# A transformer block on one core: batches in loop passes, and the same work as sixteen slots of head groups

## The chip, the core and the metric

The kernel runs on one core of one Trainium2 chip. The metric is the device time of one execution in microseconds. TensorE does matmuls, VectorE and ScalarE elementwise work and the evacuation of PSUM banks, GpSimd elementwise work in SBUF alone, and SyncE issues all DMAs. In the profile they are PE (PEld for its weight loads), DVE, ACT, POOL and SP.

## What is computed

Four batches of 512 tokens of width 512, all in float32, one pre-norm transformer block with a ternary feed-forward part:

```python
x = x + attn(layernorm(x), Wqkv, Wo)      # 16 heads of 32, causal, softmax
x = x + ffn(layernorm(x), w1, w3, w2)
# attn: scores = q @ k^T * 32**-0.5; where(causal, scores, -1e9); softmax; @ v; @ Wo
# ffn:  s = mean(|w|); wq = clip(round(w / s), -1, 1) * s   for w1, w3 (1365x512), w2 (512x1365)
#       (silu(x @ w1q^T) * (x @ w3q^T)) @ w2q^T
```

## The kernel before

**Numbers in two halves.** Each float32 operand of a large product is kept as two 16-bit floats, high and low. ScalarE writes the high half out of the bank, VectorE subtracts it from the bank and writes the low half (`turned_high` and `turned_low`, `place`, L607, L800, L808). A product of q, k, v or project then has 4 blocks x 3 terms = 12 matmuls of 512 columns (L999, L1030). The ternary weights need one half only: gate and lin have 8 matmuls, down 22 for each tile of 128 tokens (L1139).

**Attention, by groups of four heads.** A batch has four groups. For each, q and k are computed as 128 x 512 tiles (four heads of 32 rows). Their halves are stacked along the partitions, three times 32 rows for each head, so that one matmul computes all three terms: `q_stack` and `k_stack`. ScalarE copies the high half of each head into the first rows (L625), VectorE the low half (L817), and SyncE copies the first rows to a second place within SBUF (`stack`, L456, L457). Work on scores goes in ten *units* of 512 columns a group, which hold the sixteen (head, tile of 128 rows) pairs of causal widths 512, 384, 256 and 128; two units are a *piece*. There are two passes over the scores:

- `scores`: queries on partitions, two banks in turn. A matmul for each pair (L1056) and a second one that adds a large negative triangle to its last 128 columns (L1058, `mask_rows` and `mask_cols`). VectorE reduces each unit to block maxima (L829), and four small operations make the row maxima of them (L836 to L840). These are transposed (`max_row`, L1066), split, and sent by two small DMAs into two more rows of the q stack, against rows of ones (times 32768) in the k stack.
- `probs`: keys on partitions, the same products with the maximum subtracted by the extra rows (L1083), exponentials on ScalarE (L642), and GpSimd sets what is above the diagonal to zero (`select`, L558, three operations for each half of the heads).

`values` then multiplies the probabilities with v and, again, with ones for the sums (L1102, sixteen float32 products each), into `o_bank` and `sum_bank`. VectorE takes the reciprocal (L844) and the product (L850), ScalarE and GpSimd split the result (L647, L563). `project` multiplies with Wo and VectorE adds to the residual `x_res` (L856).

**The feed-forward part.** `gate` and `lin` alternate over eleven chunks of 128 hidden rows: tanh on ScalarE (L657), two scalar_tensor_tensor on VectorE (L864, L875), the halves on ScalarE (L663) and GpSimd (L568). `down` follows (L881). Statistics and normalisation are on VectorE (L733 to L743), the power -0.5 on GpSimd (L532).

**Preparation, in batch 0.** Wqkv is loaded, its largest magnitude found, and the whole is scaled and split in four blocks of 1536 columns (L600, L778). Each ternary weight is loaded into `late`; ScalarE sums the magnitudes (L673), GpSimd adds over the partitions, and then each of eleven chunks goes: VectorE rounds it (`weight_round`, L924), ScalarE takes the sign (L684), TensorE transposes (L1155, L1152), VectorE copies (L915, L913). The raw buffer of one weight is loaded anew as its chunks are done.

**The order.** `order` writes one list of steps for a pass; each engine walks through the list, doing its own part of a step, so all queues are in this order. Passes: FIRST (attention of batch 0 and preparation), MIDDLE twice in a hardware loop (attention of batch b with the feed-forward part of b-1 as *fillers*, one or two at fixed places), LAST_ATTENTION, and LAST (feed-forward of batch 3 alone). Within a pass the groups overlap: while `probs` of group g are made, so are `scores` of group g+1. At the end of a pass stand down, the next x's transposes and project; the next pass begins with q, k and v. Steps that need a bank for a product (all but scores, probs and values) take two banks, `work`, in turn (`open_work`, L986): each waits until the product before the last is evacuated. The other six banks are two for scores, two for probs, `o_bank` and `sum_bank`.

## Time and profile before

| what | us |
|---|---|
| three runs | 727.48, 727.8, 729.08 |
| median | 727.8 |
| span of the profiled execution, first to last instruction | 727.0 |
| busy: TensorE, weight loads, VectorE, ScalarE, GpSimd | 630.4, 300.6, 436.0, 335.2, 136.4 |

The profiled execution's own time isn't recorded apart from its span; the median of the runs lies 0.8 us above that span. The durations are those of single instructions from issue to end. Those of TensorE overlap, so the distance between two starts tells what one costs. The clock that the chip granted TensorE, in tenths for forty slices of 18.2 us, and the busy tenths above it:

```
PE   2695687677988999999979999999979999997998
PEclk9997888667999999999999999999999999997999
```

### The profile page before, as it was taken

To read this page: it belongs to the slowest core of one execution; us is meant where nothing else is said; L and a number is where in the kernel's file an instruction comes from. 1 tells how busy PE (TensorE), PEld (TensorE's weight loads), DVE (VectorE), ACT (ScalarE), POOL (GpSimd) and SP (SyncE) were. 2 spreads that over 40 slices of the span, in tenths; PEclk is the share of its full clock that TensorE was granted. 3 is DMA by queue.
4 is the path that set the end of the run, shared out by engine and by line. 5 is a ranking of instruction groups with operands and counts; after the bars stand their busy time and mean duration, and the time that the engine had idled before them with its cause. 6 is when DMAs were issued, how large, how long until landed. Compare 5 with 4: busy or idle time off the path is not lost.

```text
span 727.0 us, 10700 instructions
## 1 busy us (share of the span) xinstructions
PE 630.4 (87%) x3892; PEld 300.6 (41%) x3892; DVE 436.0 (60%) x816; ACT 335.2 (46%) x551; POOL 136.4 (19%) x205
## 2 busy tenths in 40 slices
PE   2695687677988999999979999999979999997998
PEld 1142333333444444444444444444434544443443
DVE  7767767974655668634575777535556775244431
ACT  2556756852345585511456555501557645202330
POOL 2000012311100233410001225401002233211330
PEclk9997888667999999999999999999999999997999
DMA  8061121300020000011100000021000000120001
GB/s 330 16 227 58 48 79 54 116 1 1 1 73 16 16 16 1 1 59 60 52 23 17 16 16 1 1 76 40 15 16 16 1 16 1 44 72 1 0 1 59
DMA packets 13930, 30.22 MB, mean 42 GB/s; under 512 B 2442, under 2 KB 2442, under 8 KB 13876
## 3 DMA queue, kind: packets, MB, share of 16 engines
q1 hardware_dynamic: 13876, 29.50, 12.8%
q8 instruction: 34, 0.56, 0.3%
q14 instruction: 20, 0.16, 0.1%
HBM read 20.97 MB, written 4.19 MB: 35 GB/s over the span
## 4 chain that ended last, share of the span: by engine, by line
PE 64%; DVE 17%; ACT 11%; issue 5%; DMA 2%; SPq 0%; POOL 0%; DVEq 0%; ACTq 0%; POOLq 0%
PE work L999 25%; PE work L1139 11%; PE work L1030 10%; PE sum_bank L1102 6%; PE o_bank L1102 4%; PE prob_bank L1083 3%; PE score_bank L1056 3%; ACT k_stack L625 3%; DVE block_max L829 3%; ACT probs L642 2%; DVE inv_sum L844 1%; ACT late L684 1%; DMA late<-in_L_ffn_w 1%; ACT late L657 1%; ACT q_stack L625 1%
## 5 line engine op out<-in xcount | busy, mean ns | idle before, releaser
L999 PE MATMUL work<-late,w_ternary 128*128 128x512 f16 (+1 forms) x704 | 168.3, 390 | 9.6 <-DVE late L864 8.1
L829 DVE TENSOR_REDUCE block_max<-score_bank 128x4 f32<-128x512 f32 x160 | 102.8, 684 | 52.3 <-PE score_bank L1058 52.2
L999 PEld LDWEIGHTS work<-late,w_ternary 128*128 128x128 f16 (+1 forms) x704 | 69.9, 102 | 90.6 <-DVE late L864 14.2
L642 ACT ACTIVATE probs<-prob_bank,scalars 128x512 f32<-128x512 f32 x160 | 100.6, 681 | 7.0 <-PE prob_bank L1083 6.0
L568 POOL TENSOR_TENSOR late<-late 128x512 f16<-128x512 f32 (+1 forms) x44 | 51.0, 1159 | 208.5 <-ACT late L663 208.5
L1139 PE MATMUL work<-w_ternary,late 128*128 128x512 f16 (+1 forms) x352 | 77.2, 379 | 0.0
L864 DVE SCALAR_TENSOR_TENSOR late<-late,work 128x512 f32<-128x512 f32 (+1 forms) x44 | 30.3, 688 | 68.7 <-ACT late L657 68.4
L1056 PE MATMUL score_bank<-k_stack,q_stack 96*128 96x512 f16 (+3 forms) x256 | 62.7, 310 | 9.3 <-DVE block_max L829 8.4
L844 DVE RECIPROCAL inv_sum<-sum_bank 128x512 f32<-128x512 f32 x16 | 53.7, 3358 | 21.5 <-PE sum_bank L1102 21.5
L1030 PE MATMUL work<-xt_hi,wqkv_hi 128*128 128x512 f16 x128 | 51.5, 402 | 17.0 <-DVE wqkv_lo L778 10.4
L647 ACT ACTIVATE ot_hi<-o_sb 128x512 f16<-128x512 f32 x16 | 10.1, 630 | 121.0 <-DVE o_sb L850 121.0
L558 POOL TENSOR_SCALAR_AFFINE_SELECT probs<-probs 128x640 f32<-128x640 f32 (+2 forms) x96 | 45.4, 504 | 82.1 <-ACT probs L642 81.8
L663 ACT ACTIVATE late<-late 128x512 f16<-128x512 f32 (+1 forms) x44 | 27.7, 630 | 64.2 <-DVE late L875 64.0
L1083 PE MATMUL prob_bank<-q_stack,k_stack 98*128 98x512 f16 (+3 forms) x256 | 53.3, 316 | 1.5 <-ACT probs L642 1.4
L1030 PE MATMUL work<-xt_lo,wqkv_hi 128*128 128x512 f16 x128 | 51.4, 402 | 0.0
L1030 PE MATMUL work<-xt_hi,wqkv_lo 128*128 128x512 f16 x128 | 51.1, 399 | 0.0
L1139 PEld LDWEIGHTS work<-w_ternary,late 128*128 128x128 f16 (+1 forms) x352 | 34.0, 98 | 41.0 <-issue 0.6
L881 DVE SCALAR_TENSOR_TENSOR x_res<-work,scalars,x_res 128x512 f32<-128x512 f32 x16 | 12.0, 751 | 62.3 <-PE work L1139 62.3
L1058 PE MATMUL score_bank<-mask_cols,mask_rows 128*128 128x128 f16 x256 | 48.7, 224 | 0.0
L618 ACT ACTIVATE half_hi<-work 128x512 f16<-128x512 f32 x32 | 19.1, 596 | 60.8 <-PE work L1030 59.0
L1102 PE MATMUL sum_bank<-probs,ones 128*32 128x128 f32 (+3 forms) x512 | 43.3, 484 | 0.2
L563 POOL TENSOR_TENSOR ot_lo<-o_sb,ot_hi 128x512 f16<-128x512 f32 x16 | 18.8, 1173 | 124.4 <-ACT ot_hi L647 117.6
(104 smaller groups left out, 911.3 us busy)
## 6 DMA issues: line engine op xcount, KB each, us to landing
late<-in_L_ffn_w SPq DMA_DIRECT2D x6, 768.0 KB, 6.5
x_res<-in_L_attn_x SPq DMA_DIRECT2D x16, 256.0 KB, 2.7
out_y<-x_res SPq DMA_DIRECT2D x16, 256.0 KB, 2.0
late<-in_L_attn_Wqkv SPq DMA_DIRECT2D x4, 768.0 KB, 8.9
xn<-in_L_attn_x SPq DMA_DIRECT2D x3, 1024.0 KB, 5.3
late<-in_L_ffn_w SPq DMA_DIRECT2D x4, 682.5 KB, 3.9
q_stack<-q_stack SPq DMA_DIRECT2D x16, 128.0 KB, 2.3
k_stack<-k_stack SPq DMA_DIRECT2D x16, 128.0 KB, 2.3
```

The source lines that it names most:

```text
L558: pool.affine_select(out=view, in_=view, compare_op=ALU.is_ge, fill=0.0, base=0, pattern=[[0, n], [1, P]], channel_multiplier=-1).then_inc ...
L568: pool.tensor_tensor(g_lo[0:m, c, :], g32[c % 2][0:m, :], g_hi[0:m, c, :], ALU.subtract).then_inc(g_lo_done, 1)
L642: act.activation(probs[:, u, :], prob_bank[u % 2][:], ACT.Exp, scale=scalar(exp_scale)).then_inc(prob_free, 1)
L829: dve.tensor_reduce(block_max[:, u, :], score_bank[u % 2][:].rearrange("p (k c) -> p k c", c=P), AX_X, ALU.max).then_inc(score_free, 1)
L844: dve.reciprocal(inv_sum[:], sum_bank[:]).then_inc(inv_done, 1)
L999: last = pe.matmul(bank, lhs, rhs, start=(n == 0), stop=(n == len(terms) - 1))
L1030: last = pe.matmul(work[s][:], w[:, c, cols], xx[:, c, :], start=(c == 0 and n == 0), stop=(c == KC - 1 and n == 2))
L1056: pe.matmul(bank[:, off:off + n], q[0:3 * HD, h, tile * P:(tile + 1) * P], k[0:3 * HD, h, 0:n], start=True, stop=False)
L1058: last = pe.matmul(bank[:, off + n - P:off + n], mask_rows[:], mask_cols[:], start=False, stop=True)
L1083: last = pe.matmul(bank[:, off:off + n], k[0:rows, h, kt * P:(kt + 1) * P], q[0:rows, h, S - n:S], start=True, stop=True)
L1102: last = pe.matmul(bank[HD * h:HD * (h + 1), S - n:S], lhs, probs[:, u, off:off + n], start=(kt == 0), stop=(kt == ST - 1), skip_group_che ...
L1139: last = pe.matmul(work[s][:], g[0:m, c, i * P:(i + 1) * P], t_down[0:m, c, :], start=(c == 0 and g is g_hi), stop=(c == HC - 1 and g is g ...
```

## The change

The passes and the hardware loop go. One list of steps, written out in full, covers all sixteen head groups (*slots*). In slot s stand the probabilities of s, the scores of s+1, the q and k products of s+2, and values and sums of s-1. The other work (preparation in slots 0 to 3; then in each batch v, project and the transposes of y in the first slot, ten of the gate and lin steps and the next x in the second, twelve in the third, down in the fourth) is spread between the pieces in proportion to given weights. Further:

- The mask is no longer a matmul. VectorE adds a float32 mask tile and takes the maximum in one instruction for each (head, tile) pair, `tensor_tensor_reduce`, whose accumulator is the row maximum. The four small operations go.
- GpSimd, after its selections, adds the probability blocks of a head (three additions for each half of the heads). TensorE's product with ones then has 2048 columns a group instead of 5120.
- The halves of q and k are stored to a DRAM buffer and read from it into all three places of the stacks, by DMA (four DMAs more for each tile). The copies L625 and L817 go. Stacks are used in turn of three. The rows of ones are set by GpSimd at the start.
- Values and sums use the `work` banks too, of which there are now four, in turn. The reciprocal is written to `o_sb`, and the product over it.
- Rounding of the ternary weights moves from VectorE to GpSimd.
- Wqkv is scaled and split by the columns that a product needs: those of q and k of group 0 first. x is loaded in four tiles, each as its buffer is free; `x_res` is loaded by steps of its own (`res_load`); `yn` has two tiles instead of four.

```diff
+NW = 4
+STACKS = 3
+STACK_ROWS = {"q": ("hi", "lo", "hi"), "k": ("hi", "hi", "lo")}
...
+def spread(anchors, fillers):
+    total, laid, out = sum(w for w, _ in fillers), 0.0, []
+    rest = list(fillers)
+    for j, anchor in enumerate(anchors):
+        out += anchor
+        while rest and laid + rest[0][0] / 2 <= total * (j + 1) / len(anchors):
+            w, steps = rest.pop(0)
+            laid += w
+            out += steps
+    for _, steps in rest:
+        out += steps
+    return out
...
+def next_x(b):
+    out = [(0.4, [("stats_x", b, i)]) for i in range(ST)]
+    out += [(0.4, [("norm_x", b, i)]) for i in range(ST)]
+    out += [(0.4, [("xt", b, i)]) for i in range(ST)]
+    return out + [(0.0, [("x_load", b + 1)])]
...
+def slot(s, early, late):
+    front = [[("scores", s + 1, 0)], [("scores", s + 1, 1)]] if s + 1 < SLOTS else [[]]
+    o = spread(front, early)
+    if s:
+        o += [("values", s - 1), ("sums", s - 1)]
+    back = []
+    for p in range(PIECES):
+        back.append([("probs", s, p)])
+        if s + 1 < SLOTS and p + 2 < PIECES:
+            back.append([("scores", s + 1, p + 2)])
+        if s + 1 < SLOTS and p == 3:
+            back.append([("max_row", s + 1)])
+    return o + spread(back, late)
+def qk(s):
+    return [(2.5, [("q", s)]), (2.5, [("k", s)])] if s < SLOTS else []
...
+def order():
+    o = [("stats_x", 0, i) for i in range(ST)] + [("norm_x", 0, i) for i in range(ST)]
+    o += [("xt", 0, i) for i in range(ST)] + [("x_load", 1)]
+    o += [("weight_scale",), ("split", 0), ("split", 1), ("q", 0), ("k", 0), ("split", 2), ("split", 3)]
+    o += [("q", 1), ("k", 1), ("split", 8)]
     for p in range(PIECES):
         o.append(("scores", 0, p))
+        o += [[("split", 4), ("split", 5)], [("v", 0, 0)], [("split", 6), ("split", 7)], [("v", 0, 1)], []][p]
+    o += [("weight_load", WEIGHTS[0], j) for j in range(PARTS)]
+    o += [("max_row", 0), ("v", 0, 2), ("v", 0, 3), ("wo_scale",), ("wo_split",)]
+    prep = preparation()
+    n = -(-len(prep) // GROUPS)
+    ups = []
+    for s in range(SLOTS):
+        b, g = divmod(s, GROUPS)
+        early, late = qk(s + 2), []
+        if b == 0:
+            late += prep[g * n:(g + 1) * n]
+        elif g == 0:
+            late += [(2.5, [("v", b, i)]) for i in range(2)]
+            late += [(2.5, [("project", b - 1, i), ("stats_y", b - 1, i)]) for i in range(ST)]
+            late += [(2.5, [("v", b, 2), ("norm_y", b - 1, 0)]), (0.4, [("yt", b - 1, 0), ("norm_y", b - 1, 1)]),
+                     (2.5, [("v", b, 3)]), (0.4, [("yt", b - 1, 1), ("norm_y", b - 1, 2)]),
+                     (0.4, [("yt", b - 1, 2), ("norm_y", b - 1, 3)]), (0.4, [("yt", b - 1, 3)])]
+            ups = ffn_up(b - 1)
+        elif g == 1:
+            late += ups[:10]
+        elif g == 2:
+            late += ups[10:]
+        else:
+            downs = 2 if b == BATCHES - 1 else ST
+            late += [(4.7, [("down", b - 1, i)] + ([("res_load", b, i - 1)] if i else [])) for i in range(downs)]
+            late.append((0.0, [("res_load", b, downs - 1)]))
+        if g == 1 and b + 1 < BATCHES:
+            late = merged(late, next_x(b + 1))
+        o += slot(s, early, late)
...
+            def place(step):
+                n, s = step
+                dst = (q_stack if n == "q" else k_stack)[s % STACKS]
+                emptied(sp, step)
+                for part_ in ("hi", "lo"):
+                    sp.dma_start(spill[n, part_], half[n, part_][:]).then_inc(spilled[n, part_], 16)
+                if s >= STACKS:
+                    sp.wait_ge(prob_full, NU * (s - STACKS + 1))
+                elif n == "k":
+                    sp.wait_ge(unit_rows_set, s + 1)
+                for part_ in ("hi", "lo"):
+                    sp.wait_ge(spilled[n, part_], 16 * (s + 1))
+                    for j in [j for j, at in enumerate(STACK_ROWS[n]) if at == part_]:
+                        sp.dma_start(dst[j * HD:(j + 1) * HD, :, :],
+                                     spill[n, part_].rearrange("(h d) s -> d h s", h=HG)).then_inc(stacked[n][s % STACKS], 16)
...
+            def select(s, pair):
+                u = 5 * pair
+                pool.wait_ge(prob_free, NU * s + u + 5)
                 blocks = probs[:, u:u + 5, :].rearrange("p u (k c) -> p (u k) c", c=P)
                 for first, step_, n in ((0, 4, 5), (7, 3, 2), (19, 1, 1)):
                     view = blocks[:, first:first + step_ * (n - 1) + 1:step_, :]
                     pool.affine_select(out=view, in_=view, compare_op=ALU.is_ge, fill=0.0, base=0,
                                        pattern=[[0, n], [1, P]], channel_multiplier=-1).then_inc(selected, 1)
+                pool.wait_ge(selected, SELECTS * s + 3 * (pair + 1))
+                sums = added[:, 2 * pair:2 * pair + 2, :]
+                n = ADDS * s + 3 * pair
+                pool.tensor_tensor(sums, probs[:, u:u + 4:3, P:S], probs[:, u + 1:u + 5:3, 0:S - P],
+                                   ALU.add).then_inc(added_done, 1)
+                pool.wait_ge(added_done, n + 1)
+                pool.tensor_tensor(sums[:, :, P:3 * P], sums[:, :, P:3 * P],
+                                   probs[:, u + 2, :].rearrange("p (h c) -> p h c", h=2), ALU.add).then_inc(added_done, 1)
+                pool.wait_ge(added_done, n + 2)
+                pool.tensor_tensor(sums[:, :, 2 * P:3 * P], sums[:, :, 2 * P:3 * P],
+                                   probs[:, u + 1:u + 5:3, S - P:S], ALU.add).then_inc(added_done, 1)
...
+            def weight_round(m, c):
+                if c == 0:
+                    pool.wait_ge(inv_made, WEIGHTS.index(m) + 1)
+                rows = HLAST if m != "w2" and c == HC - 1 else P
+                src = chunk_views(m, c)[0][0:rows]
+                pool.tensor_scalar(src, src, scalars[0:rows, inv_s[m]:inv_s[m] + 1], ROUND, ALU.mult,
+                                   ALU.add).then_inc(rounded, 1)
...
-                    dve.tensor_reduce(block_max[:, u, :], score_bank[u % 2][:].rearrange("p (k c) -> p k c", c=P),
-                                      AX_X, ALU.max).then_inc(score_free, 1)
...
+                    for j, (h, tile, off, n) in enumerate(UNITS[u]):
+                        k = NP * s + BEFORE[u] + j
+                        if k > 1:
+                            dve.wait_ge(score_free, k - 1)
+                        dve.tensor_tensor_reduce(masked[:, k % 2, 0:n], score_bank[u % 2][:, off:off + n],
+                                                 mask[:, S - n:S], 1.0, LOWEST, ALU.add, ALU.max,
+                                                 row_max[:, h, tile:tile + 1]).then_inc(score_free, 1)
...
+            def sums(step):
+                s, bank = step[1], bank_of(step)
+                full(dve, step)
+                if s:
+                    dve.wait_ge(o_lo_done, s)
+                dve.reciprocal(o_sb[:], work[bank][:]).then_inc(work_free[bank], 1)
+                emptied(dve, step)
+                before = ("values", s)
+                bank = bank_of(before)
+                full(dve, before)
+                dve.tensor_tensor(o_sb[:], work[bank][:], o_sb[:], ALU.mult).then_inc(work_free[bank], 1)
...
-                        pe.matmul(bank[:, off:off + n], q[0:3 * HD, h, tile * P:(tile + 1) * P],
-                                  k[0:3 * HD, h, 0:n], start=True, stop=False)
-                        last = pe.matmul(bank[:, off + n - P:off + n], mask_rows[:], mask_cols[:],
-                                         start=False, stop=True)
+                        last = pe.matmul(score_bank[u % 2][:, off:off + n], q[0:3 * HD, h, tile * P:(tile + 1) * P],
+                                         k[0:3 * HD, h, 0:n], start=True, stop=True)
...
-                for bank, full in ((sum_bank, sums_full), (o_bank, values_full)):
-                    for kt in range(ST):
-                        for h in range(HG):
-                            u, off, n = [(u, off, n) for u in range(NU) for hh, tile, off, n in UNITS[u]
-                                         if (hh, tile) == (h, ST - 1 - kt)][0]
-                            col = (g * HG + h) * HD
-                            lhs = ones[:] if bank is sum_bank else v_sb[:, kt, col:col + HD]
-                            last = pe.matmul(bank[HD * h:HD * (h + 1), S - n:S], lhs, probs[:, u, off:off + n],
-                                             start=(kt == 0), stop=(kt == ST - 1), skip_group_check=True)
-                    last.then_inc(full, 1)
...
+                pe.wait_ge(added_done, ADDS * (s + 1))
+                for cols in (slice(0, P), slice(P, S)):
+                    for h in range(HG):
+                        src = probs[:, 5 * (h // 2) + 3 * (h % 2), cols] if cols.start == 0 else added[:, h, :]
+                        last = pe.matmul(work[bank][HD * h:HD * (h + 1), cols], ones[:], src,
+                                         start=True, stop=True, skip_group_check=True)
+                last.then_inc(work_full[bank], 1)
...
```

The functions not shown do the same work as before with the new numbering of steps. `qk_high` and `qk_low` replace `place` on ScalarE and VectorE; each writes a 128 x 512 half.

## Rows read from the trace of the kernel before

**Rows 1.** Stretches: length, then busy us of each engine, granted clock, DMA share, GB/s.

```profile
24.70:57.70 33.00, 28.71 (x122) 11.33 (x122) 23.60 (x33) 20.64 (x29) 0.80 (x2) 1.00 0.36 125
57.70:177.40 119.70, 82.99 (x614) 40.64 (x615) 86.25 (x187) 75.94 (x126) 19.77 (x34) 0.74 0.18 54
...
335.30:492.70 157.40, 147.53 (x940) 70.58 (x940) 95.02 (x178) 71.79 (x123) 32.87 (x47) 0.99 0.10 28
...
645.60:727.00 81.40, 73.19 (x329) 33.72 (x326) 30.60 (x51) 16.87 (x26) 15.24 (x15) 0.93 0.06 21
sum 727.00, PE 630.45 PEld 300.55 DVE 435.99 ACT 335.18 POOL 136.39; mean PE 90.06 PEld 42.94 DVE 62.28 ACT 47.88 POOL 19.48
```

**Rows 2.** Timeline of the matmuls, two places: start us, duration us, engine, line, operation.

```profile
252.99 0.22 PE L1058 MATMUL score_bank<-mask_cols,mask_rows 128*128 128x128 f16 x1
253.05 0.33 PE L1056 MATMUL score_bank<-k_stack,q_stack 96*128 96x384 f16 x1
...
253.39 0.60 PE L1083 MATMUL prob_bank<-q_stack,k_stack 98*128 98x512 f16 x3
253.83 0.38 PE L1030 MATMUL work<-xt_hi,wqkv_hi 128*128 128x512 f16 x1
...
364.80 1.04 PE L1007 MATMUL work<-ident,yn 128*128 128x128 f32 x8
```

**Rows 3.** Chain of waits over the whole span: start us, us, what.

```profile
253.99 2.59 PE work L1030 x12
257.63 1.73 PE work L999 x8
...
271.79 2.29 PE sum_bank L1102 x32
274.08 2.15 PE o_bank L1102 x32
...
467.26 9.50 PE work L1139 x44
```

**Rows 4.** Groups by line and form: shapes, count, busy us, mean ns, idle before.

```profile
L829 DVE TENSOR_REDUCE block_max<-score_bank 128x4 f32<-128x512 f32 x160 | 102.8, 684 | 52.3 <-PE score_bank L1058 52.2
...
L844 DVE RECIPROCAL inv_sum<-sum_bank 128x512 f32<-128x512 f32 x16 | 53.7, 3358 | 21.5 <-PE sum_bank L1102 21.5
...
L808 DVE SCALAR_TENSOR_TENSOR half_lo<-work,half_hi 128x512 f16<-128x512 f32 x32 | 21.9, 685 | 12.5 <-ACT half_hi L618 9.5 <-issue 2.9
...
L817 DVE COPY k_stack<-half_lo 32x512 f16<-32x512 f16 x64 | 18.3, 286 | 1.7
...
L924 DVE TENSOR_SCALAR late<-late,scalars 128x512 f32<-128x512 f32 x30 | 15.7, 544 | 0.2
...
L823 DVE SCALAR_TENSOR_TENSOR max_lo<-work,max_hi 16x128 f16<-16x128 f32 x16 | 4.4, 274 | 3.3 <-ACT max_hi L636 3.3
...
L673 ACT ACTIVATION_READ_ACCUMULATOR yn<-late 128x1 f32 x12 | 2.3, 190 | 0.0
```

**Rows 5.** Costliest groups of the page, GpSimd's: busy us, mean ns of one.

```profile
L568 POOL TENSOR_TENSOR late<-late 128x512 f16<-128x512 f32 (+1 forms) x44 | 51.0, 1159 | 208.5 <-ACT late L663 208.5
...
L558 POOL TENSOR_SCALAR_AFFINE_SELECT probs<-probs 128x640 f32<-128x640 f32 (+2 forms) x96 | 45.4, 504 | 82.1 <-ACT probs L642 81.8
```

**Rows 6.** Timeline, GpSimd and VectorE at 128 us.

```profile
128.22 1.16 POOL L563 TENSOR_TENSOR ot_lo<-o_sb,ot_hi 128x512 f16<-128x512 f32 x1 [8.92 <-ACT ot_hi L647]
...
128.58 1.08 DVE L924 TENSOR_SCALAR late<-late,scalars 128x512 f32<-128x512 f32 x1
```

**Rows 7.** DMA issues: count, KB each, median us to landing.

```profile
k_stack<-k_stack SPq DMA_DIRECT2D x16, 128.0 KB, 2.3
```

**Rows 8.** Chain of waits, start of the span, ScalarE's first weights and the first probabilities.

```profile
21.13 1.58 ACT wqkv_hi L600
...
68.25 0.85 PE prob_bank L1083 x3
```

**Rows 9.** Stretches 63.5 to 168 us in four, their sum and mean.

```profile
sum 104.50, PE 75.24 PEld 37.33 DVE 75.48 ACT 70.34 POOL 18.62; mean PE 18.81 PEld 9.33 DVE 18.87 ACT 17.58 POOL 4.65
```

1130 lines of the change are left out of this document (504 added, 626 removed).

## Prediction, made before the changed kernel was run

> **What bounds the kernel now.** I read the busy time by stretch first. Its last line gives the whole span: the tensor engine works 630 of 727 us, but matmul busy counts the drain of each instruction, so it flatters [rows 1]. The stretches tell more. Up to 57.7 us lies the start. From 57.7 to 177.4 us, batch 0's attention with the preparation of the ternary weights beside it: TensorE is busy 83 of 120 us at a granted clock of 0.74, VectorE 86, ScalarE 76. From there every batch repeats at 153 to 158 us, with TensorE busy 94% at the 2.4 GHz level (granted 0.99) [rows 1].
>
> Second, the start-to-start spacing of matmuls shows what work costs at that clock. In [rows 2] a 128-column mask matmul holds the array for 0.06 us (252.99 to 253.05), though its duration reads 0.22. The probabilities of two units take 0.44 us (253.39 to 253.83). The chain of waits gives larger pieces [rows 3]: sums 2.29 us, values 2.15, a product of 12 matmuls (q, k, v or project) 2.59, a gate or lin of 8 1.73, and 44 matmuls of the down product 9.50, a pair of tiles, thus 4.75 each.
>
> So TensorE's work for one batch is: q and k 8 x 2.59 = 20.7; v 10.4; project 10.4; gate and lin 22 x 1.73 = 38.1; down 4 x 4.75 = 19.0; values and sums 4 x (2.15 + 2.29) = 17.8; probabilities, five pieces a group, 4 x 5 x 0.44 = 8.8; scores the same 8.8 and 64 masks 3.7; eight transposed tiles, two in 1.04 us [rows 2], 4; sum 141.7. A batch takes 157.4, so 15.7 us of it, 4 a head group, are gaps: now the limit is TensorE with small gaps after 177 us, and before 177 us a mix of chains.
>
> **The matmuls removed.** The mask leaves TensorE: 256 x 0.058 = 14.7 us. The sums go from 4 x (512 + 384 + 256 + 128) = 5120 columns a group to 4 x 512 = 2048 since GpSimd adds the blocks first: 2.29 x 0.4 = 0.92, less 1.37 us, times 16 = 22 us. A batch then is 141.7 - 3.7 - 5.5 = 132.5 us of work.
>
> **VectorE.** It gets 16 masked reductions a slot (head group) instead of ten reductions of 0.684 and four small ones of about 0.17 (7.5 us). No row shows this operation. Its inputs are one bank and one SBUF tile, as in the 0.685 us scalar_tensor_tensor of 512 columns; the 128-column one takes 0.274 [rows 4]. A line through both gives 4 x (0.69 + 0.55 + 0.41 + 0.27) = 7.7 us. The accumulator may be read apart: ScalarE's does, 0.19 us [rows 4], so +3.0. Bounds: 6 us (overlapped starts) and, at the reciprocal's 6.6 ns a column [rows 4], 34 us. I take 9: it is the same kind of pass as the 0.685 row. The Trainium skill (VectorE: DVE Perf Modes, section Two Vector instructions with no wait between them) says that an operation which also writes its accumulator is two instructions; by it the upper 10.7 would hold, and the sum stays.
>
> Off VectorE go the copies into the stacks (eight a slot of 0.286 us, 9.1 a batch) and, in batch 0, 33 roundings of 0.544 [rows 4]. A batch then holds VectorE for 95.0 [rows 1] - 30 + 36 - 9 = 92 of about 138 us. ScalarE loses its eight placements a slot too and has room.
>
> **GpSimd.** Two-input arithmetic costs it 1.159 us for 512 columns, the selections 96 x 0.504 [rows 5], 3.0 a slot. The adds are 768 + 512 + 256 columns for each half of the heads: 3.5 us at that rate, 7 a slot; below, at the selection's rate (504 ns for 341 columns), 2.3; above, twice the rate if blocked by VectorE, 7. I take 3.5, the row's own form. They hide behind TensorE: between the last probabilities of a slot and its sums stand some 2.4 us of filler, two score pieces 0.9, q and k 5.2, values 2.15 = 10.6 us, against exponentials 1.3, selections 1.5 and adds 3.5, 6.3 in all. Cover is lost in slots 14 and 15, which have no q and k left: 5 us in all with the end of attention. Roundings on GpSimd: 33 between 0.65 (selection rate) and 1.16 us; I take 0.9, 30 us.
>
> One tensor_scalar on VectorE took 1.08 us instead of 0.544, ending with a GpSimd operation that had begun 0.36 us before it [rows 6]. The Trainium skill (SBUF — State Buffer, section Who interferes with whom) calls the shared port pair an exclusive lock; the trace agrees. GpSimd's busy time would rise from 136 to 136 + 112 + 30 = 278 us, so VectorE's 32 normalisations meet it twice as often: at most 32 x 1 us, on the path only before the transposes of y, which my upper end holds.
>
> **The stacks** go to DRAM and come back: four DMAs more a tile. The placement within SBUF lands in 2.3 us [rows 7]; two in a row are 4.6, bounds 2.3 and 9. SyncE then issues twelve for a slot and waits between, by estimate 10 us of 33; behind these wait the maximum rows, x loads and stores. Stacks are filled one slot ahead, so TensorE doesn't wait. x loads and res_load have a slot's time too. Only in the first fill is it exposed.
>
> **Four work banks** take away waits of a product for the bank before last; the 15.7 us a batch are mostly these and the boundary between batches. Late then is VectorE's reciprocal, 3.36 + 0.69 us [rows 4], which holds the bank of the values; two products are in between. I take 1.3 us of gap a slot (bounds 0.3 and 4).
>
> **The sum**, against the profiled 727.0 us span:
> Start to the first probabilities, now 68.25 [rows 8]: w_scale is there at 21.1 in both [rows 8]; q(0) then needs only its own slice of weights (ScalarE 0.6, VectorE 0.69) and begins at 22.6, not 24.7, where the first row of [rows 1] starts. q and k 10 us (an estimate: twice 2 x 2.59, since TensorE has idled), placement 5 to 7: scores at 40. Maxima 9 and four slices of 0.69: 52. Maximum row, and its DMA behind the first weights: 57. Bounds 50 and 68.
> Slots 0 to 3: now a stretch of 104.5 / 4 = 26 us each with VectorE 18.9, TensorE 18.8, ScalarE 17.6 and GpSimd 4.7 busy [rows 9]. After: VectorE 18.9 - 4.5 - 2.3 + 1.5 = 13.6; GpSimd 4.7 + 7 + 7.5 = 19, the busiest, with rounding, sign, transpose and copy one chain. It also holds two slots' q and k of batch 1. Bounds 19 and 29; I take 25: 57 + 100 = 157.
> Slots 4 to 15 and up to the last project: three batches' work and what crosses over, 3 x 132.5 less the first scores and the q, k and x already done (about 15), plus the last values and sums 3: 385. Gaps 12 x 1.3 + 5 = 21. Together 406.
> Tail: now 81.4 [rows 1]. The transposes of y begin during the projects; the last row's chain is 5 us instead of 8.6: 78.
> 157 + 406 + 78 = 641. The measured median, 727.8, lies 0.8 over the span, so 641.5 as a run would show; I say 641.
>
> **Rivals.** (a) The chains stay: the new order closes no gap, only the matmuls go: 727 - 15 - 22 = 690. For it: VectorE and GpSimd wait in order, and a norm that waits for GpSimd's square root stands behind 5 us of selections and adds. Against: four banks and work spread evenly. (b) Better: slots 0 to 3 at 20 us, start 52, gaps 0.5 a slot: 132 + 396 + 77 = 605 to 620; for it speaks that every engine falls below 20 us a slot. (c) GpSimd's adds end late: beyond 7.8 us for half a group (2.2 times the row's rate) sums wait; at 10 us, 2.2 x 16 = 35, so 676. (d) Slower than before: the masked reduction runs at a multiple. With M us a slot, slots 0 to 3 pay M - 9 each, the other twelve M - 19 each, as VectorE's 92 - 36 = 56 a batch plus 4M then exceeds TensorE's 132. The 86 us to break even need 16M = 86 + 36 + 228, M = 21.9, 1.4 us for a piece of 320 columns on average, 4.3 ns a column; at the reciprocal's rate, M = 34, it is 641 + 100 + 180 = 921. Nothing but the reciprocal is that slow here.
>
> **Chances.** Forecast (625 to 660) 0.52; (a) 0.22; (b) 0.14; (c) 0.04; (d) 0.07; 0.01 for no change. Faster by over 0.2% (what a measurement here can tell) 0.92, within 0.01, slower 0.07. The range 606 to 692 takes in (b), (c) and (a) and the bounds of the start and of slots 0 to 3.
>
> **What would show it.** The masked reductions at about 0.7 us for 512 columns and 16 a slot; sums in about 0.9 us; start of the first probabilities near 57; projects of batch 0 from about 165 us; a batch period near 138; GpSimd near 280 us busy; waits of TensorE for added, for the banks of values, or for ternary weights name the rival. It is wrong if a masked reduction takes over 1.3 us, if TensorE waits for the adds in every slot, or if slot periods after 157 us exceed 37.

## The result, and the profile after

The changed kernel takes **759.97 us** (median of 4 runs, 758.87 to 761.48) against 728.02 us before (4 runs, 727.48 to 729.08): ratio 1.0432, 95% interval 1.0409 to 1.0455. It is 4.3% slower; I had forecast 641. The profiled execution has a span of 759.0 us.

First the stretches of the changed kernel, cut at the first probabilities, where slots 4, 8 and 12 begin, and at the last batch's first `project` (length, then busy us of each engine, granted clock, DMA share, GB/s). They answer to [rows 1], whose cuts are at the first `project` of each batch.

```profile
0.00:73.70 73.70, 39.16 (x159) 17.80 (x160) 42.16 (x94) 18.08 (x25) 10.81 (x21) 0.95 0.49 177
73.70:237.50 163.80, 94.76 (x573) 46.21 (x572) 69.56 (x216) 70.54 (x117) 70.18 (x91) 0.67 0.23 74
237.50:388.80 151.30, 138.59 (x813) 65.06 (x812) 88.06 (x219) 51.53 (x90) 63.15 (x71) 0.98 0.18 60
388.80:540.00 151.20, 138.14 (x814) 64.97 (x812) 88.28 (x219) 51.53 (x90) 63.09 (x71) 0.98 0.15 49
540.00:679.50 139.50, 120.12 (x698) 54.84 (x697) 68.62 (x149) 46.32 (x80) 61.65 (x68) 0.94 0.07 23
679.50:759.00 79.50, 72.33 (x328) 33.22 (x328) 29.71 (x50) 16.86 (x26) 15.66 (x15) 0.95 0.07 24
sum 759.00, PE 603.09 PEld 282.10 DVE 386.39 ACT 254.86 POOL 284.54; mean PE 100.52 PEld 47.02 DVE 64.40 ACT 42.48 POOL 47.42
```

The engines have about the work that I gave them: GpSimd 285 us (forecast near 280), VectorE 88 a batch (92); TensorE is busy for 603 us, 630 before. The time is lost between the work. The second line is the worst: 163.8 us in which no engine is busy for more than 95, TensorE at a granted clock of 0.67, between its two levels. A batch takes 151 us (157 before, 138 forecast). The first project's matmuls start at 243.4 us, 66 later than before and 78 later than forecast. Against the four terms of the forecast's sum: start 73.7 for 57, slots 0 to 3 163.8 for 100, slots 4 to 15 and up to the last project 442.0 for 406, tail 79.5 for 78.

The groups by form show that the prices of the single operations were right (shapes, count, busy us, mean ns, idle before). The masked reduction is called CUSTOM_DVE_ANT_0.

```profile
L791 DVE CUSTOM_DVE_ANT_0 masked<-score_bank,mask 128x512 f16<-128x512 f32 x64 | 44.0, 687 | 0.9 <-PE score_bank L988 0.6 <-issue 0.3
L791 DVE CUSTOM_DVE_ANT_0 masked<-score_bank,mask 128x128 f16<-128x128 f32 x64 | 18.3, 286 | 0.0
L791 DVE DVE_READ_ACCUMULATOR2_ANT row_max<- 128x1 f32 x256 | 21.2, 83 | 0.0
L533 POOL TENSOR_TENSOR added<-probs 128x768 f32<-128x768 f32 x32 | 58.3, 1822 | 17.0 <-issue 14.5
L562 POOL TENSOR_SCALAR late<-late,scalars 128x512 f32<-128x512 f32 x30 | 20.3, 692 | 6.9 <-issue 6.9
L1041 PE MATMUL work<-probs,ones 128*32 128x128 f32 x128 | 6.5, 274 | 4.3 <-POOL added L539 4.3
```

In two of these rows stands what I had not priced: "idle before 14.5 <-issue", 6.9 <-issue. GpSimd stood still with nothing to wait for. The chain of waits of the changed kernel at 80 us says where (start us, us, what):

```profile
83.38 1.37 POOL probs L528 x3
...
84.82 7.41 issue
92.24 1.80 POOL added L533
94.10 1.27 POOL added L536
95.44 0.72 POOL added L539
96.16 0.69 POOL late L562
96.87 1.40 ACT late L672 x2
```

The exponentials are there and the selections are made; 7.4 us pass before the first add starts, on the chain that ends last. Then GpSimd's timeline at 138 us, with the third all-reduce:

```profile
138.84 0.44 POOL L498 PARTITION_ALL_REDUCE scalars<-scalars  x1 [5.98 <-issue]
146.18 2.02 POOL L562 TENSOR_SCALAR late<-late,scalars 128x512 f32<-128x512 f32 x3 [6.89 <-issue]
```

Both ways cost: arithmetic to all-reduce 5.98 us, all-reduce to arithmetic 6.89. The selections run behind an all-reduce without such a gap, and an all-reduce itself takes 0.35 to 0.44 us. There are six gaps in the part ahead of slot 4, which I call the front: 7.5, 6.0, 6.9 and, read in the same way, 7.4 ahead of the first all-reduce, 5.7 and 7.1 ahead of 186.5 and 195.4 us. Some of this time passes while GpSimd would wait anyway (of the first gap only 3.5 us are on the path); on the chain that ends last the six stand with 3.5, 7.4, 5.7, 6.1, 4.9 and 7.0, some 35 us.

The kernel before had such gaps too, in the wait view of GpSimd (waited for: us in total, times, longest), which I had not followed up. Its other four changes of this kind lie beside waits of 5.9 to 10.9 us for VectorE or ScalarE, so the trace can't tell a gap apart there:

```profile
POOL ot_lo L563 <- issue: 6.8, 1, 6.8
POOL scalars L536 <- issue: 6.0, 1, 6.0
```

The Trainium skill (GPSIMD Engine Reference, section 2.1 Instruction dispatch) states that the first call to a freshly loaded GpSimd kernel pays about 6 us for loading its code, with no instruction visible in the profile. The traces agree in size, 5.7 to 7.5 us, and show that it comes back: at each of the six changes between these two kinds of operation in the changed kernel. That the time goes into loading code is not shown by any run here.

### The profile page after: what moved, and what is told of

Same layout as the page of the kernel before. It is cut to its first block, busy times and chain, and to the rows that moved or that the text cites. A ratio compares the mean times of both kernels' runs of the same rounds, so it can differ in the third digit from the quotient of the medians.

```text
span 759.0 us, 9353 instructions
## 1 busy us (share of the span) xinstructions
PE 603.1 (79%) x3380; PEld 282.1 (37%) x3380; DVE 386.4 (51%) x944; ACT 254.9 (34%) x428; POOL 284.5 (37%) x337
## 4 chain that ended last, share of the span: by engine, by line
PE 54%; DVE 15%; ACT 13%; issue 10%; POOL 7%; DMA 2%; SPq 0%; ACTq 0%; DVEq 0%; POOLq 0%
PE work L939 33%; PE work L1079 8%; DVE o_sb L800 6%; ACT probs L631 5%; PE work L1027 4%; PE score_bank L988 3%; PE prob_bank L1010 2%; DVE masked L791 2%; PE work L1041 2%; POOL added L533 2%; ACT late L644 2%; PE work L949 1%; ACT late L672 1%; ACT yn L660 1%; POOL probs L528 1%
## 5 line engine op out<-in xcount | busy, mean ns | idle before, releaser
L939 PE MATMUL work<-late,w_ternary 128*128 128x512 f16 (+1 forms) x704 | 162.5, 382 | 3.3 <-DVE late L839 1.8
L791 DVE CUSTOM_DVE_ANT_0 masked<-score_bank,mask 128x512 f16<-128x512 f32 (+3 forms) x256 | 111.9, 486 | 3.9 <-PE score_bank L988 3.6
L988 PE MATMUL score_bank<-k_stack,q_stack 96*128 96x512 f16 (+3 forms) x256 | 58.4, 334 | 25.2 <-DVE row_max L791 24.7
L1010 PE MATMUL prob_bank<-q_stack,k_stack 98*128 98x512 f16 (+3 forms) x256 | 57.7, 332 | 16.0 <-ACT probs L631 15.6
L800 DVE RECIPROCAL o_sb<-work 128x512 f32<-128x512 f32 x16 | 53.7, 3357 | 31.1 <-PE work L1041 31.1
L939 PE MATMUL work<-xt_hi,wqkv_hi 128*128 128x512 f16 x128 | 55.4, 433 | 16.0 <-DVE wqkv_lo L744 15.6
L533 POOL TENSOR_TENSOR added<-probs 128x768 f32<-128x768 f32 x32 | 58.3, 1822 | 17.0 <-issue 14.5
L1079 PEld LDWEIGHTS work<-w_ternary,late 128*128 128x128 f16 (+1 forms) x352 | 34.8, 100 | 42.0 <-issue 4.1
L988 PEld LDWEIGHTS score_bank<-k_stack,q_stack 96*128 96x128 f16 x256 | 24.4, 106 | 54.6 <-DVE row_max L791 36.4
L1010 PEld LDWEIGHTS prob_bank<-q_stack,k_stack 98*128 98x128 f16 x256 | 23.7, 105 | 51.6 <-ACT probs L631 26.7
L672 ACT ACTIVATE late<-late,scalars 128x512 f16<-128x512 f32 (+1 forms) x33 | 23.1, 714 | 57.9 <-POOL late L562 57.9
```

Source lines behind the costliest of these rows:

```text
L533: pool.tensor_tensor(sums, probs[:, u:u + 4:3, P:S], probs[:, u + 1:u + 5:3, 0:S - P], ALU.add).then_inc(added_done, 1)
L672: act.activation(dst, src, ACT.Sign, bias=scalar(neg_round)).then_inc(ternary_done, 1)
L791: dve.tensor_tensor_reduce(masked[:, k % 2, 0:n], score_bank[u % 2][:, off:off + n], mask[:, S - n:S], 1.0, LOWEST, ALU.add, ALU.max, row_ ...
L800: dve.reciprocal(o_sb[:], work[bank][:]).then_inc(work_free[bank], 1)
L939: last = pe.matmul(bank, lhs, rhs, start=(n == 0), stop=(n == len(terms) - 1))
L988: last = pe.matmul(score_bank[u % 2][:, off:off + n], q[0:3 * HD, h, tile * P:(tile + 1) * P], k[0:3 * HD, h, 0:n], start=True, stop=True)
```

## The experiments

Differences below are of ratios to the kernel before on the same chip, times its 728 us. Where both kernels of a pair ran four times, the two intervals together leave such a difference open by some 4 us.

**1. The all-reduces left out, in both kernels.** In `e1_no_reduce` (the changed kernel) and `e2_before_no_reduce` (the kernel before), which leave the reduction out, so that scales differ between partitions:

```diff
-                pool.partition_all_reduce(scalar(dst, n), scalar(src, n), P, op).then_inc(reduced, 1)
+                pool.tensor_scalar(scalar(dst, n), scalar(src, n), 1.0 if op == RMAX else 128.0, 0.0, ALU.mult,
+                                   ALU.add).then_inc(reduced, 1)
```

> The changed kernel with its five partition_all_reduce on GpSimd (two maxima, three sums over the partitions) replaced by a tensor_scalar of the same elements; the reduction over partitions is left out, so scales differ between partitions. Theory A (switching costs): GpSimd stands idle 5.7 to 7.5 us, with nothing to wait for, at each change between partition_all_reduce and plain arithmetic; by the trace of the changed kernel six of these lie on the path of the front (3.5 + 7.4 + 5.7 + 6.1 + 4.9 + 7.0 = 35 us) and the reductions themselves take about 2 us each more. All of it goes: 760 falls to 715 to 727. Theory B (the front is bound by its chains of weights, GpSimd to ScalarE to TensorE to VectorE): the gaps are only filled by other waits, 750 to 760. In either case the slots after 237 us stay as they are (151 us a batch).

> The kernel before with the same replacement (reduction over partitions left out). Its trace has the same idle stretches on GpSimd (6.0 and 6.8 us), but there GpSimd has nothing else urgent and the rounding is on VectorE. Theory A: 0 to 8 us faster than before (720 to 728), at least 25 us less than the replacement brings in the changed kernel. Theory B has no reason for a difference between the two: the same few us in both.

Measured: 727.8 us for the changed kernel (ratio 1.0002, 0.9984 to 1.0020), 31 us less than with them; 728.1 for the kernel before (1.0009, 0.9991 to 1.0027), nothing less. Slots 4 to 15 kept their lengths. The six gaps are gone from the wait view. So the whole of "slower than before" is five small reductions on GpSimd, free in the old kernel and 31 us in the new one. Without them the new kernel is just level, and 87 us of the forecast are still missing.

**2. The other edits on GpSimd, with the switches still in.** `e3_round_dve` puts the roundings back on VectorE, `e4_no_adds` sums all blocks on TensorE:

```diff
-                for cols in (slice(0, P), slice(P, S)):
+                for kt in range(ST):
                     for h in range(HG):
-                        src = probs[:, 5 * (h // 2) + 3 * (h % 2), cols] if cols.start == 0 else added[:, h, :]
...
+                                         probs[:, u, off:off + n], start=(kt == 0), stop=(kt == ST - 1),
```

> The changed kernel with the 33 roundings of the ternary weights back on VectorE (0.544 us each there, 0.69 on GpSimd). Theory A: after a reduction GpSimd then goes on with plain arithmetic only at the next add, so the change back is partly hidden, as in the kernel before: 760 falls by 5 to 20 us. Theory B (roundings stand behind selections and adds on GpSimd, 5 us a half group): falls by 10 to 30 us, with the gaps unchanged. A rise would say that VectorE is the busier of the two in the front.

> The changed kernel without the pre-adding on GpSimd: TensorE sums all 16 blocks of exponentials against ones, as before (2.29 instead of 0.91 us, 16 times: +22 us of TensorE), and GpSimd is freed of 7.6 us a slot. Theory A and the forecast (adds hidden): TensorE-bound slots get 1.4 us longer, +16 us for slots 4 to 15, while the front loses its gaps of 7.4 and 7.0 us ahead of the adds: 760 to 765. Theory C (GpSimd's adds are late or hold up the norms and VectorE in every slot): 760 falls to 740 or less, since each slot loses more in waits than 1.4 us.

Measured: 746.7 (1.0267), 12 less; 756.5 (1.0388), 3 less. The 12 lie in the range of both theories for `e3_round_dve`, but its trace has all six gaps still, 44.4 us in sum against 40.4 in the changed kernel, and five of them on its chain with 4.9 to 9.9 us. This speaks for theory B, roundings no longer queued behind selections and adds, and so does experiment 4, where the same edit brings 10 us with nothing switched:

```profile
POOL added L533 <- issue: 23.6, 3, 10.0
POOL scalars L498 <- issue: 20.8, 3, 9.0
```

In the wait view of `e4_no_adds` the gaps didn't go with the adds, they moved to the next arithmetic, the roundings:

```profile
POOL late L551 <- issue: 21.7, 3, 7.8
POOL scalars L498 <- issue: 20.3, 3, 7.3
```

A switch is not a property of the adds: whatever arithmetic comes next pays it. My 760 to 765 for this run was a miss. The reciprocal of slot 3 starts at 222.9 us instead of 237.0 with the gaps still there, so the adds cost something in the front besides; experiment 4 shows it without the gaps.

**3. Nothing left out, and the order of the work.** `f0_tensore_reduce` makes the reductions on TensorE; `f0_y_order` and `f0_x_early` each change one order on top of it; `f0_all_orders` has both, and moves ScalarE's copy of the finished values (`ot_hi`, with GpSimd's `ot_lo` behind it) from ahead of the next slot's exponentials to a place behind the first of them.

```diff
+                pe.matmul(work[bank][:, 0:PARTS], all_ones[:], scalar(abs_part[m], PARTS), start=True,
+                          stop=True).then_inc(work_full[bank], 1)
...
 f0_y_order, slot g == 0:
-            late += [(2.5, [("project", b - 1, i), ("stats_y", b - 1, i)]) for i in range(ST)]
-            late += [(2.5, [("v", b, 2), ("norm_y", b - 1, 0)]), (0.4, [("yt", b - 1, 0), ("norm_y", b - 1, 1)]),
...
+            late += [(2.5, [("project", y, 0), ("stats_y", y, 0)]),
+                     (2.5, [("project", y, 1), ("stats_y", y, 1), ("norm_y", y, 0)]),
+                     (2.5, [("project", y, 2), ("stats_y", y, 2), ("norm_y", y, 1)]),
+                     (0.4, [("yt", y, 0)]),
...
 f0_x_early:
+        if g == 3 and b + 2 < BATCHES:
+            late = merged(late, x_norms(b + 2))
 f0_all_orders also, in slot and then on ScalarE and GpSimd:
+        if p == 0 and s:
+            back.append([("o_hi", s - 1)])
...
-                elif step[0] == "sums":
+                elif step[0] == "o_hi":
                     values(step[1])
```

The reason for the second of these: in the changed kernel the slots of a batch take 43, 41, 35 and 32 us, from reciprocal to reciprocal, and the first holds a lockstep. Its timeline of VectorE and TensorE:

```profile
258.17 0.60 PE L949 MATMUL work<-ident,yn 128*128 128x128 f32 x4
260.12 0.54 DVE L721 TENSOR_SCALAR yn<-x_res,y_mean_var,y_rstd 128x512 f32<-128x512 f32 x1
261.64 0.61 PE L949 MATMUL work<-ident,yn 128*128 128x128 f32 x4
...
265.00 0.63 PE L949 MATMUL work<-ident,yn 128*128 128x128 f32 x4 [2.76 <-DVE yn L721]
266.90 1.23 DVE L721 TENSOR_SCALAR yn<-x_res,y_mean_var,y_rstd 128x512 f32<-128x512 f32 x1
...
268.28 1.09 PE L949 MATMUL work<-ident,yn 128*128 128x128 f32 x4 [2.65 <-DVE yn L721]
```

Transpose, norm, transpose, norm: yn has two tiles, each step frees the next, and the last norm takes 1.23 us instead of 0.54 while GpSimd adds (266.59 to 267.85).

> The changed kernel with its five reductions over the partitions moved to TensorE, so nothing of the computation is left out: a maximum is a transpose, a VectorE maximum of one row and a matmul that spreads it (two work banks); a sum is one matmul against a 128x128 tile of ones. Theory A (switching costs): as the run without any reduction, 727.8; the detours cost three or four hops of 0.3 to 0.5 us at each of the two maxima, but the 2.3 us maximum of Wo is also brought ahead of two v products: 724 to 731. Theory B (the reductions' results themselves, not the switches, were what the run without them saved): about half of the 32 us comes back, 740 to 750.

> As f0_tensore_reduce, and in the first slot of each batch's attention (43 us against some 36 us of TensorE's work) the four transposes of y stand among the projects and v products, each norm a whole product ahead of its transpose. Theory L (lockstep: norm waits for GpSimd's square root behind selections and adds, transpose waits for norm, next norm for transpose; 5 us a batch in the trace): three slots get 4 to 6 us shorter, 12 to 18 us in all against f0_tensore_reduce. Theory E (every engine is near its bound in that slot): under 4 us.

> As f0_tensore_reduce, and the statistics and normalisations of x of batches 2 and 3 are made in the fourth slot of the batch two earlier instead of in the second slot, where VectorE has ten gate and lin steps, 16 masked reductions, the reciprocal and the four xt_lo beside them. Theory V (VectorE is the bound in that slot: 40.7 us with the next x, 31.0 without it in the last batch, though TensorE's four tiles of x are only some 2 us more): two slots get 4 to 7 us shorter and the fourth, where VectorE has room, not longer by over 1: 7 to 14 us against f0_tensore_reduce. Rival: it is the transposes and their bank that cost (xt_hi on ScalarE, xt_lo on VectorE, then the bank), under 3 us.

> As f0_tensore_reduce with both reorderings, and ScalarE's copy of the finished values (ot_hi, which waits for VectorE's reciprocal and product, 4.05 us) stands behind the first exponentials of the next probabilities instead of ahead of them. If the waits are independent: the two gains add, and the copy's move brings another 0.5 to 1.5 us a slot, 8 to 24: 685 to 700 in all. If the same cover is used twice: 705 to 712.

Measured: 732.1 (1.0060), 712.5 (0.9792), 725.9 (0.9972), **690.4** (0.9477, 0.9435 to 0.9519). The reductions on TensorE cost 4 us over leaving them out, 1 more than theory A allowed and far from B. The order of y brings 19.5 us, above the 12 to 18; reciprocals of neighbouring slots, 43 us apart before, stand 36.6 apart after. That of x brings 6.4, just under the 7 to 14: its two slots fell from 40.6 to 36.4 us, with TensorE busy for 33 of them, but slot 3 took 3.1 back and the first slot of each batch 0.3 to 0.6. These slots of `f0_tensore_reduce` and of `f0_x_early`:

```profile
251.00:292.00 41.00, 34.38 (x205) 15.71 (x204) 28.29 (x68) 15.83 (x28) 19.68 (x22) 1.00 0.19 62
```
```profile
255.00:291.50 36.50, 33.16 (x204) 15.91 (x202) 21.42 (x52) 15.72 (x28) 17.15 (x18) 1.00 0.19 64
```

All together bring 42.4. The copy's move had no run of its own; if the other two keep their gains, 16.5 are left for it, inside the 8 to 24 forecast and above what the same cover used twice would leave. By the reciprocals the rest shows in the second slots of batches 1 and 2 (36.4 us in `f0_x_early`, 33.6 here), the third (34.8, 33.6) and the last slot of all (27.5, 23.2).

**4. What is left in the front.** Four single edits on `f0_all_orders`: roundings on VectorE; no adds; `LAG = 3` to 5 (the transpose that many steps behind the rounding) and the sign two steps behind it; the first two v products behind the first maximum row.

> f0_all_orders (690.4) with the 33 roundings of the ternary weights back on VectorE. Here no reduction on GpSimd is left, so nothing is switched. Theory R (in slots 0 to 3 a rounding on GpSimd stands behind 5.2 us of selections and adds, and sign, transpose and copy of the ternary weights wait for it in order on ScalarE and TensorE: 13.4 + 12.5 us of TensorE's waits): 12 to 25 us faster. Rival D (VectorE is as near to its bound in these slots): within 5 us. With the switches, the same edit brought 13.3 us.

> f0_all_orders with the sums made by TensorE from all 16 blocks and no adds on GpSimd (7.6 us a slot less there, 1.38 us a slot more on TensorE). The forecast's term: slots 4 to 15 are bound by TensorE, 12 x 1.38 = 17 us slower, slots 0 to 3 about the same: +15 to +22. Rival P (GpSimd's block of 5.2 us holds up roundings, square roots and copies): slots 0 to 3 get 3 to 5 us shorter each, which takes back 12 to 20: within 5 us of 690.4.

> f0_all_orders with the steps of the ternary weights set further apart: sign two steps behind its rounding instead of one, transpose five behind instead of three. Theory R: TensorE's 26 us of waits for the signs go down by half or more, 8 to 15 us faster. Rival D: within 3 us, since the same work in slots 0 to 3 is only waited for elsewhere.

> f0_all_orders with the first two v products behind the maximum row of slot 0 instead of between its score pieces. Its trace has four products in a row of 4.2 to 4.5 us (TensorE at its lower clock) between the scores of slot 0, so that its maxima run from 44 to 69.5 us where they hold VectorE for 9. Theory S (TensorE's own order sets the first maximum row): the first probabilities start at 64 to 68 instead of 74.3; the v products are still to be done, so of these 6 to 10 us 0 to 5 are left at the end. Rival: the start doesn't move, since the splits of the weights on VectorE and ScalarE set it.

Measured: 679.9 (0.9340), 691.8 (0.9499), 681.8 (0.9375), 691.3 (0.9502). Rounding and lag bring 10.0 and 7.4, both a little under their ranges. Without the adds it is 1.6 us slower, which can't be told from nothing, where the forecast had +15 to +22: the stretches of `all_no_adds` and of `f0_all_orders`, first slots 0 to 3, then 4 to 15 up to nearly the same step, show the two sides.

```profile
73.00:203.00 130.00, 95.44 (x650) 48.46 (x648) 74.50 (x232) 71.44 (x118) 41.17 (x68) 0.73 0.31 98
203.00:581.00 378.00, 369.44 (x2324) 178.86 (x2325) 225.58 (x561) 145.00 (x248) 91.28 (x126) 1.00 0.15 47
```
```profile
73.00:211.00 138.00, 93.63 (x580) 46.94 (x578) 74.14 (x231) 71.61 (x117) 71.33 (x92) 0.68 0.28 91
211.00:580.00 369.00, 358.22 (x2177) 173.40 (x2173) 229.67 (x561) 145.50 (x248) 173.78 (x192) 1.00 0.15 49
```

From the reciprocal of slot 3 to that of slot 15 `all_no_adds` takes 402.9 us and `f0_all_orders` 392.4: here the adds save 10.5 us, 1.3 in each slot of batches 1 and 2 but the first (0.5). That is the 1.4 of the forecast only where TensorE is the bound. Ahead of it they cost 8.6 (slot 3's reciprocal at 211.2 against 202.6), where chains bound the work and roundings stand behind blocks of 5.2 us of selections and adds on GpSimd.

The last edit failed, and so had my reading of the trace. I had taken the maxima of slot 0 to end at 69.5 us; those around 69 are slot 1's. The transpose of the finished row maxima, `max_row`, shows it in `f0_all_orders` and then in `all_v_late`:

```profile
56.94 0.27 PE L1003 MATMUL work<-ident,row_max 128*16 128x128 f32 x1 [1.35 <-DVE row_max L795]
```
```profile
53.56 0.37 PE L1004 MATMUL work<-ident,row_max 128*16 128x128 f32 x1 [0.96 <-DVE row_max L796]
```

The row came 3.4 us earlier, the first probabilities later, at 77.9 instead of 74.3. Of the products before it only one took 4.5 us, not four. Ahead of the probabilities in TensorE's order stand four v products, the first scores of slot 1 (waiting on VectorE for the split of Wo) and q and k of slot 2, in either order; with Wo's work spread out, in `comb` below, the first probabilities come at 66.9.

**5. The terms by themselves.** `comb` is `f0_all_orders` with both cures for the ternary weights, and Wo's scale and split spread over slot 0. On it: `NW = 4` to 2; the mask matmuls back beside the masked reductions; the stacks from SBUF directly.

```diff
 comb_mask:
+                        last = pe.matmul(score_bank[u % 2][:, off + n - P:off + n], mask_rows[:], mask_cols[:],
+                                         start=False, stop=True)
...
 comb_direct:
-                        sp.dma_start(dst[j * HD:(j + 1) * HD, :, :],
-                                     spill[n, part_].rearrange("(h d) s -> d h s", h=HG)).then_inc(stacked[n][s % STACKS], 16)
+                        for h in range(HG):
+                            sp.dma_start(dst[j * HD:(j + 1) * HD, h, :],
+                                         half[n, part_][h * HD:(h + 1) * HD, :]).then_inc(stacked[n][s % STACKS], 16)
```

> f0_all_orders (690.4) with the roundings on VectorE, the signs and transposes of the ternary weights further behind (lags 2 and 5), and the scale and split of Wo (a 2.3 us maximum, 2.0 us on ScalarE, 2.35 us on VectorE, ahead of slot 1's first scores now) spread over slot 0. If rounding and lag take away different waits, 690 - 10.5 - 8.7 = 671, less 2 to 4 for Wo: 667 to 672. If both take away the same waits for signs: 676 to 680.

> comb with two shared work banks instead of four. The forecast put most of the 15.7 us of gaps a batch of the kernel before down to its banks: if a product must wait for the bank before last to be emptied (ScalarE 0.6 plus VectorE 0.69, or the reciprocal's 4.05 us, which then blocks one of two banks), each slot gets 2 to 5 us longer: +30 to +80 us. If the order of the work, and not the banks, made those gaps: under +15.

> comb with the 256 mask matmuls of 128 columns put back on TensorE beside the masked reductions (the mask is added twice, the result the same). It measures the forecast's term by itself: 0.058 us each where TensorE is the bound, 3.7 us a batch, thus +11 us over slots 4 to 15, and 0 to 4 us in the front, +11 to +15. If these slots are not bound by TensorE: under +5.

> comb with the stacks filled straight from SBUF, four DMAs of 32 partitions in the place of each one from DRAM, and no spill to DRAM (24 instead of 10 DMAs a slot on SyncE's queue, but one transfer in a row instead of two, 2.3 us less in the first fill). Forecast: the way through DRAM is hidden but for the first fill, -2 to +1. Rival: issuing 24 DMAs at 0.4 to 0.8 us each takes SyncE 10 to 19 us a slot and makes the maximum rows late: +5 to +30.

Measured: **677.8** for `comb` (0.9320, 0.9275 to 0.9366), the fastest of all; 776.1 (1.0677); 686.8 (0.9434); 692.4 (0.9510). It lies 1.5 us below `all_round_dve`, within the noise; the run had been forecast at 676 to 680 if rounding and lag take away the same waits. Two banks instead of four cost 99 us, more than my upper end: the slots of a batch go from 137 to 166 us in sum. TensorE's longest waits over batch 1's slots with two banks (waited for: us in total, times, longest) are for VectorE's product behind the reciprocal, which holds one bank of two:

```profile
PE work L947 <- DVE o_sb L799: 11.0, 3, 3.7
PE work L1087 <- DVE o_sb L799: 3.7, 1, 3.7
```

These 14.7 us are half of the 29.6 that such a batch lost. In the same stretch the granted clock was 0.94, against 1.00 in `comb`:

```profile
245.00:413.00 168.00, 145.25 (x818) 66.67 (x815) 89.72 (x219) 52.52 (x90) 63.27 (x71) 0.94 0.16 52
```

So the 99 us are the waits and the lower clock that came with them; they were not taken apart.

The masks cost 8.3 us (11 to 15 expected; reciprocals stand 35, 35, 34, 37 apart instead of 34, 34, 33, 36, up to 1 us a slot). The direct stacks cost 13.8, in the rival's range. But from slot 3's reciprocal to slot 15's they take 392.4 us against 390.8, so nearly all of it is lost in the front: later slots hide either route. The DRAM route is the cheaper one in the first fill as well; in `comb_direct` the first scores start at 46.1 us instead of 38.2, behind this wait:

```profile
PE score_bank L993 <- DMA k_stack<-k_lo: 7.9, 1, 7.9
```

SyncE's queue in `comb_direct` and in `comb`, the first q and k:

```profile
29.51 5.04 SPq L441 DMA_DIRECT2D q_stack<-q_hi  x8
34.59 2.49 SPq L441 DMA_DIRECT2D q_stack<-q_lo  x4
37.20 4.95 SPq L441 DMA_DIRECT2D k_stack<-k_hi  x8
42.19 2.49 SPq L441 DMA_DIRECT2D k_stack<-k_lo  x4
```
```profile
31.93 0.43 SPq L443 DMA_DIRECT2D q_stack<-q_lo_spill  x1
32.40 0.43 SPq L435 DMA_DIRECT2D k_hi_spill<-k_hi  x1
...
34.69 0.80 SPq L443 DMA_DIRECT2D k_stack<-k_hi_spill  x2
35.53 0.43 SPq L443 DMA_DIRECT2D k_stack<-k_lo_spill  x1
```

24 issues of 0.6 us put the end of the last one at 44.7 us instead of 36.0.

## Why the prediction was wrong

Of the 119 us between 641 and 760 the runs name some 81 (31, 42 and 11, less the 4 that the reductions cost on TensorE). The steps that failed:

- **GpSimd's adds "hide behind TensorE", and its roundings cost only their own 30 us: 31 us, the step that turned the sign.** I priced GpSimd by the sum of its instructions, and that sum was right (285 us for 278). I gave nothing for going from all-reduce to arithmetic and back. In the old kernel this was free because little else on GpSimd was urgent; the change put adds and roundings, on which ScalarE and TensorE wait, right behind each all-reduce. The cover was gone, and I had not asked what it covered. "Slower" had a chance of 0.07 in the prediction, all of it for a slow masked reduction, which ran at the forecast's rate.
- **"I take 1.3 us of gap a slot", 42 us.** The four banks do what I said and more (99 us between two and four). But I took banks to be the cause of nearly all gaps. The order had its own: the lockstep of norms and transposes (19.5 us), x beside a busy VectorE (6.4), and, as the rest of 42.4 and not by a run of its own, ScalarE's copy ahead of the exponentials (16.5). Rival (a) had named the first of these mechanisms and rested on the wrong sum, since its 690 assumed the old gaps and nothing new. With the orders mended a batch takes 136.5 us in `comb` (below), the 138 of the forecast.
- **Slots 0 to 3 at 25 us each, with rounding, sign, transpose and copy of the ternary weights as one chain: 11 us shown by `comb`.** The rest of this stretch stays: 134 us against 100.
- **The start at 57.** I followed the chain of slot 0 alone and left out what stands ahead of the first probabilities in TensorE's order. They come at 73.7, in `comb` at 66.9; by `all_v_late` it is not the maximum row that sets it.

The stretches of `comb`, cut like those above at first probabilities, slots 4, 8 and 12, and the last batch's first project:

```profile
0.00:66.90 66.90, 38.69 (x163) 18.24 (x164) 37.71 (x91) 16.19 (x24) 10.24 (x20) 0.95 0.55 194
66.90:201.00 134.10, 93.41 (x592) 47.92 (x591) 99.57 (x272) 74.61 (x120) 53.56 (x59) 0.71 0.31 97
201.00:337.50 136.50, 133.49 (x813) 64.82 (x812) 88.63 (x219) 52.70 (x90) 63.29 (x71) 1.00 0.19 61
...
595.30:675.40 80.10, 72.71 (x328) 33.10 (x328) 29.71 (x50) 16.87 (x26) 15.66 (x15) 0.96 0.07 24
```

Against the terms of the sum: 66.9 for 57, 134.1 for 100, 394.3 (201.0 to 595.3) for 406, 80.1 for 78. So `comb` is 44 us above the forecast ahead of slot 4 and 12 below it behind, and that its total is only 37 above is in part luck: two errors of opposite sign. Ahead of slot 4 VectorE is busy 99.6 of 134 us and TensorE 93.4 at a granted clock of 0.71. Of the four pairs of q and k products in it q takes 3.5, 2.6, 4.4 and 4.2 us and k 2.6 each time, as both do later. How much of the 34 us is this clock and how much the chains that go with it was not tried apart, and the cause of the rest of this stretch stays open; I had priced its matmuls as if they ran at the upper level, 2.4 GHz.

What held: the masked reduction (7.8 us a slot without its accumulator reads, 0.687 for 512 columns against my 0.69) and with it the fall of rival (d); sums in 0.91 us; the stacks hidden behind a slot (1.7 us of difference between the two routes over slots 4 to 15); the tail (79.5 against 78). Too large were the gains of masks (8 us of 14.7) and adds (10.5 of 16.4 in slots 4 to 15, next to nothing in sum): matmul time was saved in full (1.0 of 0.9 us and 1.3 of 1.4 a slot) only in slots that TensorE bounds. One reading of the prediction was inexact: in [rows 6] VectorE's slow operation ends 0.3 us behind GpSimd's, not with it; nothing in the sum hangs on that.

## What to carry to other kernels

Before giving an engine more work, read why it stands idle now: an idle stretch with nothing to wait for is a cost that its slack is hiding, and it is paid as soon as other engines wait for that engine. Price a rewritten order by walking each in-order queue through one slot (what stands ahead of this instruction, what it waits for, who waits behind it), not by the sums of work; here the work of GpSimd and VectorE was forecast to within 5% and the time wrong by 19%. Then mend the order before judging the parts: on the same arithmetic it was worth 42 us, and with the reductions off GpSimd it turned a kernel 4.3% slower into one 5.2% faster.

## What the runs showed of the hardware

- In the changed kernel GpSimd stands still 5.7 to 7.5 us at each of the six changes between PARTITION_ALL_REDUCE and TENSOR_TENSOR or TENSOR_SCALAR, in both directions; in `e4_no_adds` up to 7.8, in `e3_round_dve` once each 9.0 and 10.0. The time runs beside a wait for another engine (of the first 7.4 us only 3.5 were on the path). Affine selections started 0.0 to 0.1 us behind an all-reduce.
- The same small reductions over the partitions made on TensorE (one matmul with ones, or transpose, maximum and spreading matmul) cost 4 us for all five over leaving them out, with the maximum of Wo taken somewhat earlier.
- The masked reduction runs at the rate of a plain one (687 ns for 512 columns, 684 in the kernel before); its accumulator read of 83 ns mostly overlaps the next instruction.
- A DMA of 32 partitions within SBUF keeps SyncE's queue 0.6 us, a spill or a refill through DRAM 0.4; with 24 of the first the scores started 7.9 us later than with 10 of the second.
- While GpSimd added, one normalisation on VectorE took 1.23 us instead of 0.54.
